# A mixture-of-experts layer behind gated attention: routing on capped logits, three one-hot blocks moved to ScalarE, dummy matmuls and the weight table moved

## The reference

```
x = x + tanh(g_xattn) * mlstm(layernorm(x), ctx, ctx)
t = layernorm(x).reshape(1024, 256)
logits  = 30 * tanh((t @ w_gate) / 30)              # capped, [1024, 8]
probs   = softmax(logits)
mask    = one_hot(top_k(probs, 2)).sum(-2)
weights = probs * mask
out = sum over e of (silu(t @ w1[e]) * (t @ w3[e])) @ w2[e] * weights[:, e]
x = x + tanh(g_ffn) * out
```

## Time and profile before

| what | us |
|---|---|
| median of 3 runs | 229.91 (229.88 to 231.53) |
| the profiled execution | 229.46 |
| its span, first to last instruction | 227.7 |
| TensorE busy (matmuls) | 197.8 |
| VectorE busy | 129.8 |
| ScalarE busy | 111.9 |
| POOL busy | 88.8 |

### The profile page before, as it was taken

How to read it: one execution, slowest core, us unless ns; L and a number is a source line. 1 busy time by engine, 2 the same in 40 slices (tenths; PEclk the granted TensorE clock), 3 DMA queues, 4 the chain that set the end, 5 groups by cost and what they waited for, 6 DMA issues and landing times.

```text
span 227.7 us, 4241 instructions
## 1 busy us (share of the span) xinstructions
PE 197.8 (87%) x1331; PEld 146.4 (64%) x1332; DVE 129.8 (57%) x310; ACT 111.9 (49%) x224; POOL 88.8 (39%) x96
## 2 busy tenths in 40 slices
PE   8999899898978712769999999999999999999940
PEld 2488544444436511557888888888888888888830
DVE  6897574679899878976777852223323222222310
ACT  2478888898855795026666622233223322223210
POOL 8100343365740000510445646555444555453222
PEclk9999999999999855699999999999999999999997
DMA  3999999901011140210232233333333322334222
GB/s 117 313 367 376 371 373 374 342 24 49 0 49 46 46 153 33 62 33 1 44 53 46 46 49 46 50 55 61 57 58 42 50 46 46 46 52 62 27 23 23
DMA packets 20032, 23.41 MB, mean 103 GB/s; under 512 B 3888, under 2 KB 15152, under 8 KB 20016
## 3 DMA queue, kind: packets, MB, share of 16 engines
q1 hardware_dynamic: 13696, 16.94, 21.6%
q0 software_dynamic: 4464, 6.16, 17.2%
q10 hardware_dynamic: 1856, 0.10, 0.5%
HBM read 17.95 MB, written 5.24 MB: 102 GB/s over the span
## 4 chain that ended last, share of the span: by engine, by line
PE 74%; DVE 12%; ACT 5%; issue 4%; DMA 2%; POOL 1%; DVEq 0%; POOLq 0%; ACTq 0%
PE bank L1335 28%; PE bank L1352 17%; PE bank L1164 6%; PE bank L1061 4%; PE bank L1344 4%; PE bank L1204 3%; ACT arena L487 2%; PE bank L1317 2%; PE bank L1085 2%; DMA out_dram<-hraw,sidx 2%; PE bank L1180 2%; DVE arena L787 1%; DVE vp L968 1%; PE bank L1184 1%; PE bank L1228 1%
## 5 line engine op out<-in xcount | busy, mean ns | idle before, releaser
L447 POOL DMA_INDIRECT out_dram<-hraw,sidx x23 | 37.6, 1636 | 63.1 <-DVE hraw L1021 57.2
L1335 PE MATMUL bank<-arena_r,xn_sb_r 128*128 x184 | 57.2, 392 | 0.0
L1015 DVE TENSOR_TENSOR x_sb<-x_sb,bank 128x512 f32<-128x512 f32 x23 | 15.8, 688 | 57.5 <-ACT x_sb L637 57.5
L1352 PE MATMUL bank<-w_sb,xn_sb 128*128 x184 | 43.6, 380 | 0.8 <-ACT xn_sb L641 0.8
L1335 PEld LDWEIGHTS bank<-arena_r,xn_sb_r 128*128 128x128 f32 x184 | 34.6, 188 | 7.1
L1335 PE MATMUL bank<-w_sb_r,xn_sb_r 128*128 x92 | 38.2, 415 | 0.8 <-issue 0.6
L637 ACT ACTIVATE x_sb<-bank 128x512 f32<-128x512 f32 x23 | 13.7, 598 | 49.5 <-PE bank L1335 49.5
L1352 PEld LDWEIGHTS bank<-w_sb,xn_sb 128*128 128x128 f32 x184 | 33.2, 190 | 4.6 <-issue 1.0
L408 POOL TENSOR_SCALAR_AFFINE_SELECT arena<-arena 128x1024 f32<-128x1024 f32 x16 | 17.7, 1104 | 36.6 <-ACT arena L517 36.6
L641 ACT ACTIVATE xn_sb<-bank 128x512 f32<-128x512 f32 x23 | 13.7, 598 | 25.8 <-PE bank L1344 25.8
L787 DVE TENSOR_TENSOR arena<-bank,arena 128x1024 f32<-128x1024 f32 x16 | 19.6, 1222 | 7.0 <-POOL arena L408 6.8
(11 more groups left out here) (206 smaller groups left out, 257.8 us busy)
## 6 DMA issues: line engine op xcount, KB each, us to landing
w_sb<-in_L_ffn_w_dram SPq DMA_DIRECT2D x24, 512.0 KB, 9.3
x_sb<-in_x_dram SPq DMA_DIRECT2D x2, 512.0 KB, 6.7
arena<-in_ctx_dram SPq DMA_DIRECT2D x2, 512.0 KB, 9.3
out_dram<-x_sb SPq DMA_DIRECT2D x8, 128.0 KB, 1.8
xnorm_scratch<-xn_sb SPq DMA_DIRECT2D x8, 128.0 KB, 1.7
out_dram<-hraw,sidx POOLq DMA_INDIRECT x23, 3.8
cvT<-xnorm_scratch,gidx POOLq DMA_INDIRECT x12
hraw<-xnorm_scratch,gidx POOLq DMA_INDIRECT x11, 2.9
```

The source lines that it names most:

```text
L447: nc.gpsimd.indirect_dma_start(out=out[:, :], out_offset=bass.IndirectOffsetOnAxis(ap=sidx[:, i:i + 1], axis=0), in_=y_sb[i % 2], in_offse ...
L1335: last = nc.tensor.matmul(ps_scores[p][:, n, :], a, w, start=(k == 0 and j == 0), stop=(k == KC - 1 and j == 2))
L1352: last = nc.tensor.matmul(ps_tr[:, 0:H], hT_sb[p][:, k * P:(k + 1) * P], w2_sb[:, bass.ds(e * W2 + k * H, H)], start=(k == 0), stop=(k == ...
```

## The change

- ScalarE's Tanh signals by itself (`s_th`), and VectorE's top 2 runs on the capped logits `lt` in place of `ex`. The exponentials of the two chosen logits are made by ScalarE (`wtop`, 128x16) behind the normalized tokens and ahead of the load of the Silu set.
- `lower_weights(0, 1)` moves from in front of the top 2 to in front of `lower_weights(0, 3)`.
- VectorE builds blocks 0 to 7 and 8 to 12 of `oh_r`, in two operations. It copies the three last slots as floats (`slotf`), and ScalarE makes blocks 13 to 15 with Abs(slot - column) and Relu(1 - that), an Abs and a Relu for each block, in front of the upper weights of expert 1. The token table's matmuls wait for these one by one.
- TensorE gets two dummy matmuls in front of `logits(3)`, and eight right behind the token table; the 4 + 8 + 8 in front of `turn_x(0)` and the function `warm_up_r` go.
- `weight_table()` moves from in front of `gate_up(0)` to behind `turn_x(1)`. On VectorE, `lower_x(0)` comes in front of the scatter indices (`token_slots()`) and the weight selectors (`select_weights()`), and `split(1)` in front of `slot_weights()`.

```diff
@@ constants
+    LATE_OH = 3
...
+        SOME = (0, 8, NS - LATE_OH)
+        slotd = carve(zrow, [P] * 2)
@@ ScalarE
-            follow(nc.scalar.activation(lt..., lt..., ACT.Tanh, scale=1.0 / SOFTCAP))
+            nc.scalar.activation(lt..., lt..., ACT.Tanh, scale=1.0 / SOFTCAP).then_inc(s_th, 1)
+            act.wait_ge(s_th, 1)
             nc.scalar.activation(ex[:], lt[:], ACT.Exp, scale=SOFTCAP).then_inc(s_exl, 1)
...
+            act.wait_ge(s_top, 2)
+            nc.scalar.activation(wtop[:], r8[:, 0:TOPK, :], ACT.Exp, scale=SOFTCAP).then_inc(s_exl, 1)
             nc.scalar.preload_act_table_set("silu_and_others")
+            act.wait_ge(s_dump, 16)
+            act.wait_ge(s_slf, 1)
+            for n in range(LATE_OH):
+                follow(nc.scalar.activation(slotd[n % 2], iota_r[:], ACT.Abs, scale=-1.0, bias=slotf[:, n:n + 1]))
+                nc.scalar.activation(oh_r[:, NS - LATE_OH + n, :], slotd[n % 2], ACT.Relu, scale=-1.0,
+                                     bias=one_c[:, 0:1]).then_inc(s_ohl, 1)
@@ VectorE
-            lower_weights(0, 1)
...
-            dve.wait_ge(s_exl, 1)
-            src = ex
+            dve.wait_ge(s_th, 1)
+            src = lt
             for k in range(TOPK):
-                link(nc.vector.tensor_reduce(r8[:, k, :], src[:], AX_X, ALU.max))
+                nc.vector.tensor_reduce(r8[:, k, :], src[:], AX_X, ALU.max).then_inc(s_top, 1)
+                dve.wait_ge(s_top, k + 1)
...
+            nc.vector.tensor_copy(slotf[:], sloti[:, 1, NS - LATE_OH:]).then_inc(s_slf, 1)
...
-            for q in range(4):
-                n4 = slice(q * NS // 4, (q + 1) * NS // 4)
+            for q in range(2):
+                some = slice(*SOME[q:q + 2])
...
+            lower_weights(0, 1)
             lower_weights(0, 3)
 
+            dve.wait_ge(s_exl, 2)
...
             lower_x(0, 0)
+            token_slots()
+            select_weights()
+            split(1)
             slot_weights()
-            split(1)
             hidden(0, 0)
@@ TensorE
             turn_x2(3)
+            warm_up(2)
             logits(3)
...
             for n in range(NS):
-                if n % (NS // 4) == 0:
-                    pe.wait_ge(s_sel, n // (NS // 4) + 2)
+                if n in SOME[:2]:
+                    pe.wait_ge(s_sel, SOME.index(n) + 2)
+                if n >= SOME[2]:
+                    pe.wait_ge(s_ohl, n - SOME[2] + 1)
...
             last.then_inc(s_tab, 1)
+            warm_up(8)
...
-            warm_up(4)
-            warm_up_r(8, 2 * P)
-            warm_up_r(8, P)
             turn_x(0, s_xg[0], 16, 0)
-            weight_table()
             gate_up(0, 0, expert_of(0), 0)
             turn_x(1, s_xg[1], 16, 1, 1)
+            weight_table()
             turn_h(0, 0, False)
```

More of the change, by code:

```diff
@@ L173, in bass_gated_mlstm_moe_kernel @@
         etf = sb("etf", [P, NT])
+        slotf = sb("slotf", [P, LATE_OH])
+        wtop = sb("wtop", [P, TOPK, B])
         tab = sb("tab", [P, 5, NT])
@@ L282, in bass_gated_mlstm_moe_kernel @@
         s_lg = sem("logits_done")
-        s_exl = sem("router_exp_done")
+        s_th = sem("capped_logits_done")
+        s_top = sem("top_logits_found")
+        s_exl = sem("router_exps_done")
+        s_slf = sem("late_slots_copied")
+        s_ohl = sem("late_slot_selectors_done")
         s_mask = sem("mask_done")
@@ L622, in _ @@
             act.wait_ge(s_lt, 1)
-            follow(nc.scalar.activation(lt.rearrange("p b e -> p (b e)"), lt.rearrange("p b e -> p (b e)"), ACT.Tanh,
-                                        scale=1.0 / SOFTCAP))
+            nc.scalar.activation(lt.rearrange("p b e -> p (b e)"), lt.rearrange("p b e -> p (b e)"), ACT.Tanh,
+                                 scale=1.0 / SOFTCAP).then_inc(s_th, 1)
+            act.wait_ge(s_th, 1)
             nc.scalar.activation(ex[:], lt[:], ACT.Exp, scale=SOFTCAP).then_inc(s_exl, 1)
@@ L935, in _ @@
                 if k == 0:
-                    link(nc.vector.scalar_tensor_tensor(out=ex2[:], in0=oh[:, 0], scalar=-BIG, in1=ex[:],
+                    link(nc.vector.scalar_tensor_tensor(out=ex2[:], in0=oh[:, 0], scalar=-BIG, in1=lt[:],
                                                         op0=ALU.mult, op1=ALU.add))
@@ L965, in _ @@
                                     ALU.mult).then_inc(s_sel, 1)
-            for q in range(4):
-                n4 = slice(q * NS // 4, (q + 1) * NS // 4)
-                nc.vector.tensor_tensor(oh_r[:, n4], iota_r[:, :].unsqueeze(1).to_broadcast([P, NS // 4, P]),
-                                        sloti[:, 1, n4].unsqueeze(2).to_broadcast([P, NS // 4, P]),
+            for q in range(2):
+                some = slice(*SOME[q:q + 2])
+                m = SOME[q + 1] - SOME[q]
+                nc.vector.tensor_tensor(oh_r[:, some], iota_r[:, :].unsqueeze(1).to_broadcast([P, m, P]),
+                                        sloti[:, 1, some].unsqueeze(2).to_broadcast([P, m, P]),
                                         ALU.is_equal).then_inc(s_sel, 1)
@@ L982, in _ @@
             link(nc.vector.tensor_scalar(r8[:, 4, :], r8[:, 4, :], tg[:, 1:2], None, ALU.mult))
-            link(nc.vector.tensor_tensor(wsel[:], r8[:, 0:TOPK, :],
+            link(nc.vector.tensor_tensor(wsel[:], wtop[:],
                                          r8[:, 4, :].unsqueeze(1).to_broadcast([P, TOPK, B]), ALU.mult))
@@ L990, in _, with token_slots, select_weights @@
             link(nc.vector.tensor_copy(wpart[:, 2, :], wres[:, 1, :]))
[L991 to L999, removed]
+            def token_slots():
+                link(nc.vector.tensor_copy(tab[:, 0:2, :].rearrange("p g t -> p (g t)"), ps_small[:, 256:256 + 2 * NT]))
+                link(nc.vector.tensor_scalar(tokf[:, 1, :], tab[:, 1, :], -1.0, 1.0, ALU.mult, ALU.add))
+                link(nc.vector.scalar_tensor_tensor(out=tokf[:, 1, :], in0=tokf[:, 1, :], scalar=dump[:, 0:1],
+                                                    in1=tab[:, 0, :], op0=ALU.mult, op1=ALU.add))
+                nc.vector.tensor_copy(sidx[:], tokf[:, 1, :]).then_inc(s_idx, 1)
+            def select_weights():
+                for j in range(3):
+                    nc.vector.tensor_tensor(wsl[:, :, j, :], sel[:, :, 1, :], nt(wpart[:, j, :]),
+                                            ALU.mult).then_inc(s_wsl, 1)
             def slot_weights():
@@ L1061, in warm_up @@
                     nc.tensor.matmul(ps_ht[:, :], ones_b[:], ones_b[:, :].unsqueeze(1).to_broadcast([P, 4, P]),
[L1062 to L1068, removed]
                                      start=True, stop=True)
```

## The result

The changed kernel took 228.38 us in the median (227.59 to 229.90, 8 runs) against 230.06 for the kernel before (229.52 to 231.53, 8 runs). The ratio is 0.9927, with a 95% interval of 0.9903 to 0.9951: 1.7 us less, less than 1%. The two together say 0.5%, about 1.1 us. Ratios leave out executions that lie over 1.5% above the fastest of the same kernel, such as two of 339 and 687 us in e7 and one of 689 us in e12.

The account below looks back on a forecast made before the run. The prediction took a chain of waits through routing and the first expert tiles as the bound. Token table 0.9 earlier, tile 1's gates 1.95 earlier in all: 229.91 - 1.95 = 227.96, say 228.0; own range 227.4 to 228.6, overall 227.0 to 229.9.

Parts of the forecast that it names:

- What bounds the kernel: Chain through routing and first expert tiles; edits are worth how far tile 1's gates move; clock low about 80 to 97.
- Routing, 0.60: VectorE's first top-2 step needs Tanh alone and starts at 80.71 instead of 81.31: gain 0.60 us.
- the bound of 0.71: First top-2 step: if the unexplained issue gap vanishes, it starts at 80.60, gain 0.71 us.
- The unexplained 0.37: Gap before VectorE's first top-2 step, 80.94 to 81.31, called issue; the forecast moved it along with VectorE's own work.
- One-hot blocks, net 0.21: Three blocks on ScalarE: VectorE's selectors gain 0.52, slot copy costs 0.09, four more table matmuls 0.22; net gain 0.21 us.
- The 1380 ns of drain: Skill page's extra cost per ScalarE table load; by it blocks end near 90.3 and the token table comes 0.4 later.
- Logits dummies, 0.1: Two dummy matmuls before the last logits: range -0.2 to 0.47 us, taken as 0.1 gain.
- The bound by the table load: ScalarE's table load ends at 79.83; Tanh (80.30) can't come before it, so the logits dummies gain at most 0.47.
- the 0.80: Last logits: eight matmuls took 1.86 us against 1.06 for the same eight earlier; full rate would be 0.80 earlier.
- Behind the table: New order after the token table at 90.1: tile 0's gates at 94.9, tile 1's at 101.7, 1.95 us earlier.
- the tie within 0.1: Before tile 0's gates: TensorE's upper part of x (94.45) and VectorE's weights chain (94.4) finish together within 0.1.
- Rival 1: Half rate in tile 0's gates, or a clock fall before tile 1's, takes about 1.15 back: 229.1; chance 0.34.

Follow-up runs that it names:

- e7: Changed kernel with six more dummy matmuls between the weight table and tile 0's hidden transposes; 229.44 us, ratio 0.9955 to the kernel before.
- e12: Kernel before with more dummies around its logits: six in place of four before the second logits, three before the last transposes; ratio 0.9991.
- e2: Changed kernel with all 16 one-hot blocks on VectorE, in two operations of 8, and no slot copy; 229.26 us, ratio 0.9952.
- e10: Changed kernel with more dummies around the logits and four between tile 0's transposes and gates, expert number loaded ahead of them; 228.23 us, ratio 0.9943.
- e5: Changed kernel without the two dummy matmuls in front of the last logits; 228.81 us, ratio 0.9950 to the kernel before.
- e6: Changed kernel without the eight dummy matmuls behind the token table; 230.08 us, ratio 1.0009 to the kernel before.
- e8: Changed kernel with another VectorE order: tile 0's hidden product ahead of expert 1's fourth lower weight and the slot weights; 228.34 us, ratio 0.9917.
- e9: Changed kernel measured again, unaltered, against the kernel before; 228.99 us, ratio 0.9978 (0.9951 to 1.0004).
- e1: Kernel before with the routing part alone: top 2 on capped logits, separate exponentials, expert 0's lower-weights product moved; 231.11 us, ratio 1.0034.
- e11: Changed kernel with the edits of both e8 and e10; 226.03 us, ratio 0.9854 to the kernel before, five executions.
- e4: Changed kernel with the old 4 + 8 + 8 dummies before tile 0's transposes, none right behind the table; 230.66 us, ratio 1.0006.
- e3: Changed kernel with the weight table before tile 0's gates again, VectorE's selectors and indices before the lower part of x; 231.73 us, ratio 1.0051.

## Why the prediction was right

The forecast was 228.0 us, range 227.0 to 229.9, and the median 228.38 came out; the forecast gain of 1.95 stands against 1.7 in the first measurement and 0.5 in the second. So the steps were right, and that the median came within 0.4 us of the forecast is in part luck: 228.99 came out the second time. Point by point:

- **What bounds the kernel.** Right: the last column of the table moves by 0.8 us over fourteen profiles, and the gates of tile 1 by 6.2. One reading of the earlier trace rows was off, and entered no sum: the four low slices span 74.0 to 96.7, not about 80 to 97.
- **Routing, 0.60.** The first top-2 step comes 0.61 behind the scaled logits instead of 1.27: 0.66, between the forecast and the bound of 0.71. The unexplained 0.37 shrank to a wait that ends 0.09 behind Tanh. The first step of the loop then costs 0.15 more, with 0.18 us idle behind it that the kernel before doesn't have, so the mask gains 0.51.
- **One-hot blocks, net 0.21.** From the mask to the table 6.84 became 6.53: 0.31. The selectors took 1.95 (forecast 1.97); the eight last matmuls 0.49, not 0.56. ScalarE ended at 90.84 and VectorE at 91.34: slack 0.5, as forecast. Against the rule of the Trainium skill ("ScalarE: Activation LUTs", Rules for kernel authors), e2 has the table 0.33 later with everything on VectorE. The 1380 ns of drain (the Trainium skill, same page, What ACT_TABLE_LOAD costs) are not seen here either: in e10 the load ends at 80.53 and Tanh starts at 80.55.
- **Logits dummies, 0.1.** Not resolved: e5 lies between the two ratios of the changed kernel. The bound by the table load is real, as e10 shows: with the logits at full rate the first distance is 0.34 longer, which takes back 0.34 of the 0.80 and leaves 0.46, the bound of the forecast. But the load is not fixed at 79.83: in e10 it ends at 80.53.
- **Behind the table.** Forecast 4.8 to the gates of tile 0 and 11.6 to those of tile 1, measured 5.02 and 11.68. The gather, called not bound, was mis-sized: it lands 2.83 us after its issue, not 2.4, so it and not the dummies releases the transposes, 0.24 us behind them. That cost nothing here, as these start 3.43 behind the table, forecast 3.45. The 0.2 us more lie behind them, in the lower part of x (4.45 behind the table, forecast 4.35) and in the 0.15 from its end to the gates. VectorE was free for it at 96.23 and ScalarE done with the upper part at 96.27: the tie within 0.1 of the forecast. Fewer dummies would not bring the transposes forward, since without any (e6) they start 3.39 behind the table. The weight table is done at 100.7 and VectorE asks at 101.3: hidden by 0.6, as forecast.
- **The sum by steps.** 0.82 to the table and 0.98 behind it are 1.8 us; forecast were 0.9 (with 0.1 of the logits) and 1.05.
- **Rival 1.** It is no rival but a part of the truth, in some executions and not in others. Of the six profiles with the eight dummies and nothing behind them (changed, e2, e5, e7, e8, e9) two have the gates of tile 0 at half rate (in e7 the clock rose at 93.0 and fell again at 96.4, in e2 it did not rise before 98.7), with 12.86 and 12.76 behind the table in place of 11.68: 1.1 to 1.2, against 1.15 forecast. Its other half, a fall ahead of tile 1's gates, shows in no profile. On average it takes back some 0.4 of the 1.8. The remaining 0.3 or so, down to the 1.1 that two measurements give together, stays open; the place of the fall near the logits, which moves the scaled logits from 79.2 to 82.1, is the largest scatter in it. It does not seem to favour one kernel: the mean clock over all executions is 0.947 for the changed kernel (20) and 0.946 for the kernel before (107, of the measurements beside e1 to e12). At 0.940 to 0.947 their medians are 229.16 and 229.92, at 0.954 to 0.957 they are 228.27 and 229.39: 0.8 to 1.1 us apart at like clock, though not always on the same chip.

## What to carry to other kernels

Find the one start behind which the chain no longer changes, and price every edit by how far it moves that start; here it held for fourteen kernels within 0.8 us, while spans scattered by the clock. An early part pays only if nothing behind it takes it up: the routing alone (e1) lost its 0.5 us to the product moved into VectorE's chain, and with the logits held (e12) a fixed row of filler was late. Where the granted clock decides, compare its mean in each execution before the medians. Look at the idle stretch right ahead of the dense matmuls, not only at the one behind the last work: in both profiles with four dummies there and the register load in front of them (e10, e11) the gates ran at full rate, in two of six without them they did not. What these four bring alone was not measured.

## What the hardware did that I had not expected

- The same instructions in the same order met the fall of the clock at different points of the program: about 71 us in the profiles of the changed kernel, e4 and e9, at 75.4 to 78.2 in those of before, e1, e2, e5 to e8; in e3 it fell at 70.5, rose at 74 and fell again at 80.8. (With more dummies it fell at 80.2 in e10 and 81.8 in e11, and in e12 as in e3.) The scaled logits of the changed kernel and its variants moved from 79.2 (e3) to 82.1 (e9) with it. Two stretches of the same first half, of e9 and then of e8:

```profile
70.00:72.00 2.00, 2.00 (x14) 1.58 (x14) 1.87 (x5) 0.93 (x3) 0.00 (x0) 0.71 0.00 0
```

```profile
70.00:72.00 2.00, 2.00 (x15) 1.38 (x15) 1.85 (x5) 0.93 (x3) 0.00 (x0) 1.00 0.00 0
```

- A slower clock does not only stretch work. Through dummies of a fixed number it moves what stands behind them: sixteen fp32r dummies took 2.93, 3.51, 3.69 and 3.87 us in four profiles.
- Longer gates cost less than their length where another engine is late: 1.25 us on the chain for 1.6 us in e6.
